# Vision tower with experts on one core: the first two experts' tokens placed by one-hot products

## The reference

```python
h = tokens(x)                                     # patches, two layer norms, positions, class tokens
h = h + attention0(layernorm(h))                  # 16 heads, causal, weights quantized to 5 levels
h = h + tanh(layernorm(h) @ W @ A1 @ A2 + bias)
h = h + attention1(layernorm(h))                  # 16 heads, biases, head mask
h = h + experts(layernorm(h))

def experts(x):
    xf = x.reshape(-1, 256)                       # 1216 tokens
    cap = 76                                      # 1216 / 16 experts
    score = softmax(xf @ Wg + bg)
    gate, idx = max(score), argmax(score)
    pos = rank of the token among those of its expert
    keep = pos < cap
    buf[idx, pos] = xf where keep                 # (16, 76, 256)
    h = relu(buf @ W1 + b1)                       # 256 -> 1024 per expert
    y = h @ W2 + b2                               # 1024 -> 256 per expert
    return where(keep, y[idx, pos] * gate, 0)
```

## Time and profile before

| | us |
|---|---|
| median of three runs | 352.74 |
| lowest and highest | 350.38, 354.98 |
| the profiled execution | 351.94 |
| its span, first to last instruction | 350.1 |
| TensorE busy in it | 327.1 |
| VectorE, ScalarE, POOL busy | 196.7, 170.9, 168.6 |

### The profile page before, as it was taken

One profiled execution on the slowest core, in us unless ns is written; L12 is line 12 of the kernel. 1 busy time (PEld: TensorE's weight loads), 2 busy tenths in 40 slices (PEclk: granted clock), 3 DMA queues, 4 the chain that ended last, 5 costly groups with the idle time before them and its releaser, 6 DMA issues.

```text
span 350.1 us, 8930 instructions
## 1 busy us (share of the span) xinstructions
PE 327.1 (93%) x3254; PEld 235.7 (67%) x3254; DVE 196.7 (56%) x516; ACT 170.9 (49%) x483; POOL 168.6 (48%) x289
## 2 busy tenths in 40 slices
PE   4978999979999999999999999969999999999993
PEld 3857777767878888878788778757455454464461
DVE  4458868527477866596746788750333361361350
ACT  0579725645555666567575556630342342350340
POOL 2147549866576967489884775661002012012012
PEclk9998999989999999999999999969999999999997
DMA  7999014333155649275112134116999998993400
GB/s 225 415 394 411 28 33 168 110 106 103 60 169 169 219 150 296 71 220 205 57 46 81 61 105 155 58 44 206 388 385 408 347 383 338 344 336 115 136 11 13
DMA packets 40155, 66.24 MB, mean 189 GB/s; under 512 B 4831, under 2 KB 30920, under 8 KB 39760
## 3 DMA queue, kind: packets, MB, share of 16 engines
q1 hardware_dynamic: 35832, 56.37, 46.7%
q10 hardware_dynamic: 2632, 7.05, 5.3%
q0 software_dynamic: 1648, 2.24, 1.9%
HBM read 54.17 MB, written 8.48 MB: 179 GB/s over the span
## 4 chain that ended last, share of the span: by engine, by line
PE 83%; SPq 6%; DMA 4%; issue 3%; POOL 2%; ACT 1%; DVE 0%; POOLq 0%; ACTq 0%
PE bank L1110 12%; PE bank L1077 12%; PE bank L965 8%; PE bank L941 6%; PE bank L1016 6%; SPq L741 5%; PE bank L1005 5%; PE bank L1032 5%; PE bank L995 5%; PE bank L976 5%; PE bank L1039 4%; PE bank L1088 4%; PE bank L950 3%; PE bank L1022 2%; PE bank L899 1%
## 5 line engine op out<-in xcount | busy, mean ns | idle before, releaser
L866 POOL DMA_INDIRECT out<-mid,idx x12 | 11.7, 978 | 97.7 <-DVE mid L1480 97.7
L1110 PE MATMUL bank<-early,mid 128*64 128x256 f32 (+1 forms) x448 | 43.7, 381 | 0.0
L824 POOL TENSOR_TENSOR mid<-mid,tab 128x608 f32<-128x608 f32 x32 | 38.5, 1209 | 9.5 <-PE bank L995 8.8
L1270 ACT ACTIVATE mid<-bank,cols 128x64 f32<-128x64 f32 (+1 forms) x128 | 25.9, 333 | 25.1 <-PE bank L1088 25.1
L1077 PE MATMUL bank<-early,mid 128*64 128x512 f32 (+1 forms) x192 | 36.2, 596 | 0.7 <-ACT mid L1253 0.7
L965 PE MATMUL bank<-xnT,attn 128*128 128x256 f32 (+1 forms) x160 | 36.3, 381 | 0.0
L1110 PEld LDWEIGHTS bank<-early,mid 128*64 128x64 f32 (+1 forms) x448 | 25.3, 123 | 15.8 <-issue 2.9
L1392 DVE TENSOR_REDUCE mx<-bank 102x16 f32<-102x608 f32 x32 | 25.1, 784 | 17.4 <-PE bank L995 16.9
L965 PEld LDWEIGHTS bank<-xnT,attn 128*128 128x128 f32 x160 | 29.8, 195 | 4.6 <-issue 1.1
L809 POOL TENSOR_TENSOR rs<-rs,mhalf 128x1 f32<-128x1 f32 (+2 forms) x50 | 29.0, 579 | 4.2
L941 PE MATMUL bank<-early 128*128 128x256 f32 (+2 forms) x120 | 28.3, 397 | 0.0
(11 more groups left out here) (150 smaller groups left out, 657.3 us busy)
## 6 DMA issues: line engine op xcount, KB each, us to landing
early<-in_w SPq DMA_DIRECT2D x52, 512.0 KB, 7.4
v3a<-vt SPq DMA_DIRECT2D x102, 40.0 KB
early<-vt SPq DMA_DIRECT2D x90, 40.0 KB
expert_in<-k_empty SPq DMA_DIRECT2D x6, 514.0 KB, 4.0
early<-in_xf SPq DMA_DIRECT2D x4, 768.0 KB, 16.2
early<-in_xt ACTq DMA_DIRECT2D x4, 768.0 KB, 23.1
xnT<-in_w SPq DMA_DIRECT2D x4, 512.0 KB
tokens<-in_w SPq DMA_DIRECT2D x4, 512.0 KB
```

The lines of the kernel that those rows point to most:

```text
L824: eng.tensor_tensor(km[:, n % 2], bc(kT[:, :, n * PCOLS:(n + 1) * PCOLS], 2, 4), bc(bc(quarterm[:, :], 2, PCOLS), 1, KC), ALU.mult).then_i ...
L1110: ins = mm(Yp[m % 2][a * width:(a + 1) * width, 0:DIM], hT[:, m % 2, c, a * width:(a + 1) * width], w2s[e % W2_SLOTS][:, c, :], start=c == ...
L1270: ins = eng.activation(hT[:, m % 2, c, a * width:(a + 1) * width], Tp[0][:, c * 128 + a * width:c * 128 + (a + 1) * width], ACT.Relu, bias ...
```

## The change

Experts 0 and 1 (rows 0 to 127 of the slots, the first pair tile) no longer reach TensorE by way of DRAM. For each token tile VectorE compares the tile's slot number with the numbers 0 to 127, which gives a matrix `place` of tokens by slots with a single one per row (step `eq`; `numbers` is a new constant of 64 KB, loaded behind `attn1`). TensorE multiplies the tile's normed rows by it and adds up over the ten tiles in PSUM (`gx`, into `Sp`). The sum is the turned tile that ScalarE copies to `xeT`. The scatter of all rows and all twelve loads stay, since the residual rows and the other experts need them. SyncE now issues all twelve, tile 2 first. The 29 constant products are gone. `first_half(0)`, `turn_hidden(0)` and `hidden(0)` stand ahead of the turning of the next tiles. The tables of the planner are new: `GOAL`, the paces, the cost of `bs`, and the arrival times, of which a few lines stand here.

```diff
-PAIR, TILE, LAYER, EAGER = 6.69, 9.27, 112.7, 1000
+PAIR, TILE, LAYER, EAGER = 6.69, 7.68, 110.5, 922.8
...
-XARRIVES = [9.2, 11.5, 16.5, 22.5, 27.0, 31.5]
+XARRIVES = [12.0, 16.4, 21.2, 27.8, 30.5, 37.6]
...
+        step("dve", "eq", 0, t, ("dve", "cnt", 0, t), *([("pe", "gx", 0, t - 4)] if t > 3 else []))
+        step("pe", "gx", 0, t, ("dve", "eq", 0, t), ("dve", "s", 1, PAIRS - 1))
...
+        numbers = sb("numbers", [128, 128], U32)
+        place = fv[:, :, :].rearrange("p b n -> p (b n)").rearrange("p (b n) -> p b n", b=4)
...
                     sp.dma_start(attn1[:, :], i["in_attn1"]).then_inc(l_attn1, 16)
+                    sp.dma_start(numbers[:, :], k["k_numbers"]).then_inc(l_numbers, 16)
...
-            for t in range(0, XTILES, 2):
+            for t in [2, 1, 0, *range(3, XTILES)]:
                 sp.dma_start(xe[:, t, :], xbuf[128 * xrow[t]:128 * xrow[t] + 128, :]).then_inc(xe_loaded[t], 16)
...
             sp.wait_ge(stored, 16 * TILES)
+            sp.wait_ge(pair_taken, 1)
             first(5)
...
+                elif kind == "gx":
+
+                    r = rows(n)
+                    if n == 0:
+                        pe.wait_ge(p_ready, 2 * PAIRS)
+                    pe.wait_ge(placed, n + 1)
+                    for kc in range(KC):
+                        ins = mm(Sp[:, kc, 0:128], xnd[0:r, n, kc * 128:(kc + 1) * 128], place[0:r, n % 4, :], start=n == 0, stop=n == TILES - 1, skip_group_check=True)
+                    ins.then_inc(spread, 1)
...
-            pe.wait_ge(p_ready, 2 * PAIRS)
-            for n in range(29):
-                mm(Sp[:, n % 2, 0:128], ones[:, :], ident[:, :], start=True, stop=True)
+            first_half(0)
             for use in last_uses:
                 emptied(pe, use)
-            turn(Yp[0], pair_tile(0)).then_inc(pair_turned, 1)
-            first_half(0)
+            turn_hidden(0)
             turn(Yp[1], pair_tile(1)).then_inc(pair_turned, 1)
             turn(Yp[0], late_tile(0)).then_inc(late_turned, 1)
...
                 first_half(3 * g + 1)
-                turn_hidden(3 * g)
+                if g:
+                    turn_hidden(3 * g)
...
-            act.wait_ge(scattered, 16 * TILES)
-            for t in range(1, XTILES, 2):
-                act.dma_start(xe[:, t, :], xbuf[128 * xrow[t]:128 * xrow[t] + 128, :]).then_inc(xe_loaded[t], 16)
...
+            act.wait_ge(spread, TILES)
+            eng.copy(xeT[:, 0:2, :, 0:MAIN].rearrange("p e k n -> p k e n"), Sp[:, :, 0:128].rearrange("p k (e n) -> p k e n", e=2)).then_inc(pair_taken, 1)
+            stage(0)
+            hidden(0)
             act.wait_ge(pair_turned, 1)
-            take_pair(Yp[0], 0, 1)
-            stage(0)
-            act.wait_ge(pair_turned, 2)
             take_pair(Yp[1], 1, 1)
...
+                elif kind == "eq":
+
+                    dve.wait_ge(slots_ready, n + 1)
+                    if n == 0:
+                        dve.wait_ge(l_numbers, 16)
+                    if n >= 4:
+                        dve.wait_ge(spread, n - 3)
+                    eng.tensor_tensor(place[0:r, n % 4, :], numbers[0:r, :], sloti[0:r, n:n + 1].to_broadcast([r, 128]), ALU.is_equal).then_inc(placed, 1)
```

32 lines of the change are left out of this document (19 added, 13 removed), and 7 rows, old and new, of the table GOAL.

## The result

The changed kernel takes 354.98 us (median of 20 runs, 352.67 to 359.38), the kernel before 351.48 us (20 runs, 349.37 to 355.64). The ratio is 1.010, with a 95% interval of 1.0075 to 1.0125: the change costs 1%, some 3.5 us. Forecast were 347.6 us and a range up to 353.0. The profiled execution of after took 356.03 us (span 354.2), 4.1 us more than that of before.

The account below looks back on a forecast made before the run. Bound: TensorE work in the attention body, then a five-engine latency chain. T moves -1.7 and +3.9 us; the first expert product gains 6.8, mostly lost at the second, leaving 4.3: 351.94 - 4.3 = 347.6 us, range 343.5 to 353.0.

Parts of the forecast that it names:

- From 253.24 the chain is TensorE alone: From `first_half(2)` to the end: whatever starts earlier there ends earlier, if weights keep up; 4.3 us gain carried through.
- The rival on late transfers: At `first_half(4)`: weights of experts 6 and 7 come late, DMA becomes the bound, 348.9 us; chance 0.05.
- Term 1: Front: T, the end of the last attention projection, comes 1.7 us earlier through a shorter TensorE wait at 73.16 us.
- Term 2: Ahead of the last attention projection's end: six one-hot products, a router product and two counts add 3.9 us on TensorE.
- Term 3: From the last attention projection to the first expert product: `first_half(0)` starts at 236.6 instead of 243.42.
- Term 4: Second expert product: gather, low clock and ScalarE's activations take back most of 6.8 us; `first_half(1)` 3.3 us earlier, total gain 4.3.
- The first rival: First two expert products: TensorE stays at the low clock through both, 7.3 us each, 353.8 us; chance 0.06.
- The moved gathers: SyncE's queue: twelve issues take 6 us on one queue; only issue time differs, nothing in the sum hangs on it.

Follow-up runs that it names:

- e5: Kernel before with its order kept, bias block ahead of the gathers, ten one-hot compares and products put in by hand; ratio to the kernel before 1.0004.
- e1: Changed kernel with the late experts' bias block loaded ahead of the gathers on SyncE's queue; ratio to the kernel before 1.0008.
- e16: e1 again, word for word, on another chip; ratio to the kernel before 1.0025.
- e12: e9 with the bias block back behind the weights of experts 4 and 5; ratio to the kernel before 1.0112.
- e2: Kernel before with only the planner's new numbers, no one-hot work, fillers and gather as before; ratio to the kernel before 1.0137.
- e13: Kernel before with the planner's new numbers and the bias block ahead of the gathers, no one-hot path; ratio to the kernel before 1.0153.
- e11: Kernel before with only the bias block moved ahead of the gathers, a control; ratio to the kernel before 0.9967.
- e7: e6 with the second pair's turn and copy ahead of `turn_hidden(0)` and `hidden(0)`; ratio to the kernel before 0.9961.
- e8: e1 with twelve filler products in TensorE's waits between the last attention projection and `first_half(0)`; ratio to the kernel before 0.9961.
- e6: e1 with one-hot products 7 and 8 moved behind the last count on TensorE; ratio to the kernel before 0.9977.
- e4: Changed kernel with the six odd-tile gathers back on ScalarE's queue, behind its `stage(0)`; ratio to the kernel before 1.0143.
- e9: Changed kernel with the edits of e1, e6 and e7 and nine fillers together; ratio to the kernel before 0.9946.

## Where the prediction was right and wrong

**"From 253.24 the chain is TensorE alone, so whatever `first_half(2)` gains there, the end gains too, as long as weights keep up."** This step failed first. The chain of waits shows what ended last, not what ended 1.6 us earlier. The late block was on VectorE with a wait of 2.67 us, one view away, and it hangs on the last scatter: gather plus 24.15. By the prediction's own numbers (scatter landed at 239.0) the residual would have come at 263.15, `second_half(2)` at 264.4, and TensorE wanted it at 266.0 - 4.3 = 261.7: 2.7 of the 4.3 us gone, 350.3. The rival on late transfers had the right resource and the wrong one of its transfers: it counted the bias block's 0.52 MB among the bytes ahead of W1 of experts 6 and 7, and did not ask who waits for the block itself. At `first_half(4)`, where it looked, only e5's profile has a wait, 0.56 us. Its chance of 0.05 was far too small. e1, e16 and e12 price the block's place at 0.8 to 1.7%.

**Term 1, T 1.7 us earlier.** Wrong in sign. The gap at 73 us closed but for a wait of 0.73 us at 70.1, and others opened at 104 to 122 us. At the same clock of the front, e2 has T 1.25 later than before, and e13 3.23 later than e11 (226.33, with a wait of 3.27 us at 71.26 that is 0.7 to 1.5 us in the eleven other profiles of the new order); the table of four cells prices the order at 0.4 to 0.6% with the path. This is the second failed step.

**Term 2, 3.9 us of work ahead of T.** Right in kind, a little too large. With the front's clock at 0.91, e7, e8 and e12 have T at 229.04, 227.39 and 229.65, mean 228.7, and e2 225.85: 2.85 us. Together the two terms gave 226.8 where 228.7 is measured at that clock. The remaining 1.5 us of the profiled execution's 230.25 go with its front, at 0.83. The compare took 0.29 us (0.27 forecast).

**Term 3, slots at T + 8.5, `first_half(0)` at T + 9.8.** Too early: 10.15 and 12.22 were measured. The walk left out that the new order has two products ahead of the last count (2.08 us, behind a wait of 0.61). Where they stand behind it, in e6, slots come at T + 8.66: the rest of the walk held. The products behind then run at the low level, which the walk had at 0.55 for one.

**Term 4.** Held. The lull took the clock to its low level, 0.56 from 240 to 245.8 us, `first_half(0)` took 4.92 us (5.2 forecast), 7.60 us lie between the first two products (8.0), 4.39 between the next two (4.3), and the activations were what the second waited for (e7). By the trace and by e8 the low level is paid, about 0.9 us of `first_half(1)`'s start. The Trainium skill, page "TensorE: Matmul & The Clock Gate" (The HAM clock gate), has activity release the throttle, and e8's rows agree: with the fillers the clock was back at 240.20, when `first_half(0)` began. The first rival did not come true in the changed kernel; in e4 both products ran partly at the low level, 5.33 and 5.35 us where it had 7.3 for each.

**The moved gathers.** "Nothing in the sum hangs on it" held for the issuers: 24.54 us on two queues, 24.61 on one. The Trainium skill, "DMA: Bandwidth & Descriptors" (Issuing engines are not separate DMA queues), has all issuers share the same DMA engines, and by these two numbers the traces agree. What did matter was the order on the queue.

The way from 1 to the measured 1.0100 can be walked over the kernels: before with the block early 0.9967, the path in the old order 0.9968, the new order with the path 1.0017 (mean of e1 and e16), the block behind 1.0100. That makes shares of -0.33%, 0.01%, 0.49% and 0.83%. They add up by construction, each is known to a few tenths of a percent only, and since order and path don't add up (e13), the shares of these two depend on the order of steps. Against the forecast of -1.2%, the block's place is the largest single step and the order the second; the gain of the path itself, 1.3 to 1.4% in the new order, was there, but only against what the new order costs without it.

## What to carry to other kernels

A chain of waits names the work that ended last; before a gain on it is booked, look on the other engines for waits that ended a few microseconds earlier, and ask on what they hang: here on the same scatter that the change was to hide. Where an operation that an engine waits for comes last in a DMA queue only because it was written last, its place is worth trying first; the gain depends on whether anything waits for it (0.8% in e1, nothing to be seen from e2 to e13). When a new order closes a gap, count the busy time of every stretch after it, since the order that closes one wait can open others.

## What the runs showed that was not expected

T goes with the front's clock, in the new order. From 20 to 40 us, where TensorE partly waits for images, the granted clock is 0.83, 0.91 or 1.00, even among kernels whose front is the same program (all with the new order). T follows: 230.3 in the mean at 0.83 (after, e4, e9), 228.7 at 0.91, 227.1 at 1.00 (e1, e6, e16). Some 2.2 of these 3.2 us are there when the first score products run (54.4 us at 1.00, 56.2 to 56.9 at 0.83). In the old order nothing of the kind is seen: the seven profiles have these products at 58.9 to 59.3 us, at 0.91 and 1.00 alike. That the clock is the cause, and not a companion of late images, is not shown. With one profile of each kernel, differences of T under 3 us in the new order say little before the clock of the front is looked at.

A wait of 4.62 us in the midst of dense work cost about 7: 2.4 us more for the products behind it, at the lower clock (e12). One of 2.74 us (after) brought no such loss: the 64 matmuls behind it took 3.66 us.

A VectorE operation can wait inside its own row. In e5 two of the ten compares took 1.25 and 1.18 us, the others 0.28 to 0.30. Both had begun while POOL worked on its `km` product, and ended with it. Timeline of POOL and VectorE in e5:

```profile
197.50 1.21 POOL L856 TENSOR_TENSOR mid<-mid,tab 128x608 f32<-128x608 f32 x1
197.60 1.25 DVE L1488 TENSOR_TENSOR fv<-numbers,sloti 128x128 f32<-128x128 uint32 x1
```

The Trainium skill, "SBUF — State Buffer" (SBUF: two separate sides), has VectorE and GpSimd share a pair of ports that the first holds for its whole instruction, against a VectorE operation with two inputs in SBUF and a GpSimd operation that reads SBUF. These rows agree: the compare has two such inputs, and the `km` product reads SBUF. So the cover of a compare is not VectorE's idle time alone, but also POOL's.
